# Two mixtures of experts in one kernel: routing weights spread by DMAs that repeat a DRAM row, and inputs laid out by the host

## What is computed

```python
x = x + tanh(g_xattn[0]) * strided_cross_attention(layernorm(x), ctx)         # 16 heads
x = x + tanh(g_ffn[0])   * (attention + mixture_0)(layernorm(x))
x = x + tanh(g_xattn[1]) * bidirectional_match(layernorm(x), ctx)
x = x + tanh(g_ffn[1])   * mixture_1(layernorm(x))

# mixture_0: 8 experts, hidden width 256, best two by softmax, and a shared expert
combine = sum(one_hot(topi, 8) * softmax(topw))
spec = einsum('etd,te->td', (silu(gate) * up) @ e_down, combine)
out = X + swiglu(h2, sh_gate, sh_up, sh_down) + spec
# mixture_1: 16 experts, hidden width 64, best two, weights summed to 1
y = sum(y_sel * scores)
y = y + sigmoid(xt @ Wsg.T) * (silu(xt @ Ws_gate.T) * (xt @ Ws_up.T)) @ Ws_down.T
```

## Time and profile before

| | us |
|---|---|
| three runs | 495.77, 496.0, 497.8 (median 496.0) |
| span of the profiled execution | 494.2 |
| PE busy | 453.3 |
| DVE busy | 358.1 |
| POOL busy | 319.0 |
| ACT busy | 287.7 |
| DMA queue of SP and ACT, share of 16 engines' span | 6.9% and 0.2% |

### The profile page before, as it was taken

One profiled execution on the slowest core, in us unless ns is written; L12 is line 12 of the kernel. 1 busy time (PEld: TensorE's weight loads), 2 busy tenths in 40 slices (PEclk: granted clock), 3 DMA queues, 4 the chain that ended last, 5 costly groups with the idle time before them and its releaser, 6 DMA issues.

```text
span 494.2 us, 11017 instructions
## 1 busy us (share of the span) xinstructions
PE 453.3 (92%) x3724; PEld 341.0 (69%) x3724; DVE 358.1 (72%) x930; ACT 287.7 (58%) x559; POOL 319.0 (65%) x525
## 2 busy tenths in 40 slices
PE   6859888999999999999999999899989997899996
PEld 5646555676677777677767877686858775687674
DVE  4657877899988878968656747775766756877864
ACT  2424566766787774565674476536664477446452
POOL 7895889898868676546934584547635573446553
PEclk9988999999999999999999999999999999999999
DMA  6340000040101000020000000000000000000000
GB/s 164 79 140 2 0 3 3 1 119 5 56 3 57 1 1 0 1 55 0 2 1 0 2 1 1 0 0 0 0 0 1 2 1 0 23 1 23 0 23 21
DMA packets 19353, 9.80 MB, mean 20 GB/s; under 512 B 6535, under 2 KB 18792, under 8 KB 19304
## 3 DMA queue, kind: packets, MB, share of 16 engines
q1 hardware_dynamic: 18584, 9.04, 6.9%
q10 hardware_dynamic: 720, 0.13, 0.2%
HBM read 8.12 MB, written 1.05 MB: 19 GB/s over the span
## 4 chain that ended last, share of the span: by engine, by line
PE 49%; POOL 18%; DVE 14%; issue 13%; ACT 4%; POOLq 1%; ACTq 0%; DVEq 0%
PE PS L1774 9%; PE PS L1776 9%; PE PS L1775 8%; POOL HLO L618 3%; DVE work L1382 2%; PE PS L1700 2%; PE PS L1694 2%; PE PS L1930 2%; DVE work L1387 2%; PE PS L1689 2%; PE PS L1662 2%; PE PS L1734 2%; POOL rs L437 1%; DVE RDT L1135 1%; PE PS L1677 1%
## 5 line engine op out<-in xcount | busy, mean ns | idle before, releaser
L618 POOL TENSOR_TENSOR HLO<-work,HHI 128x512 fp32r<-128x512 f32 x111 | 143.1, 1292 | 128.2 <-ACT HHI L869 124.8
L876 ACT ACTIVATE work<-PS 128x512 f32<-128x512 f32 x112 | 66.8, 596 | 91.1 <-PE PS L1776 88.4
L1382 DVE TENSOR_TENSOR work<-work,PS 128x512 f32<-128x512 f32 x104 | 71.0, 683 | 57.3 <-ACT work L876 32.3
L1387 DVE TENSOR_TENSOR work<-PS,work 128x512 f32<-128x512 f32 x112 | 77.2, 691 | 19.2 <-POOL HLO L618 10.8
L869 ACT ACTIVATE HHI<-work 128x512 fp32r<-128x512 f32 x111 | 69.8, 629 | 29.3 <-DVE work L1387 29.1
L1099 DVE TENSOR_REDUCE nmax<-PS 128x4 f32<-128x512 f32 x64 | 42.2, 683 | 8.3 <-PE PS L1662 7.9
L738 ACT ACTIVATE EX<-PS 128x512 f32<-128x512 f32 x64 | 35.0, 603 | 12.3 <-PE PS L1677 12.1
L1774 PE MATMUL PS<-HHI,W0H_down 128*128 128x512 f32 x72 | 35.0, 485 | 0.2
L1774 PE MATMUL PS<-H2H,W0H_gate 128*128 128x512 f32 (+1 forms) x72 | 32.0, 444 | 0.7 <-ACT work L876 0.7
L1930 PE MATMUL PS<-CWT,sel 128*128 128x512 bf16 (+1 forms) x68 | 26.5, 390 | 6.5 <-DVE work L1382 6.0
L1774 PE MATMUL PS<-H2H,W0H_up 128*128 128x512 f32 (+1 forms) x72 | 29.2, 406 | 2.9 <-DVE work L1387 2.9
(11 more groups left out here) (355 smaller groups left out, 1204.3 us busy)
## 6 DMA issues: line engine op xcount, KB each, us to landing
X<-in_x_dram SPq DMA_DIRECT2D x4, 256.0 KB, 5.2
raw<-in_L_ffn_e_gate_dram SPq DMA_DIRECT2D x1, 1024.0 KB, 5.5
raw<-in_L_ffn_e_up_dram SPq DMA_DIRECT2D x1, 1024.0 KB, 7.2
out_dram<-X SPq DMA_DIRECT2D x3, 256.0 KB, 2.3
raw<-in_L_ffn_We_gate_dram SPq DMA_DIRECT2D x1, 512.0 KB, 4.0
raw<-in_L_ffn_We_up_dram SPq DMA_DIRECT2D x1, 512.0 KB, 3.9
raw<-in_L_ffn_We_down_dram SPq DMA_DIRECT2D x1, 512.0 KB, 4.1
ctx_nat<-in_ctx_dram SPq DMA_DIRECT2D x1, 462.0 KB
```

The lines of the kernel that those rows point to most:

```text
L618: pool.tensor_tensor(HLO[t][:], HH[k % 2][:], HHI[t][:].bitcast(F32), ALU.subtract).then_inc(m_sem["lo"], 1)
L876: act.activation(SG[c % 2][:], PS[:, c % 2, :], ACT.Silu).then_inc(S["silu"], 1)
L1382: dve.tensor_tensor(SG[c % 2][:], SG[c % 2][:], PS[:, 4, :], ALU.mult).then_inc(S["scaled"], 1)
L1387: dve.tensor_tensor(HH[c % 2][:], PS[:, 2 + c % 2, :], SG[c % 2][:], ALU.mult).then_inc(S["hid"], 1)
```

## The change

**Spreading.** The pieces, the selectors and the selector products are gone. PE transposes `comb` itself in float32 (8 or 17 rows x 512), ACT copies it to one tile `CW`, SP stores it to a DRAM tensor `WD[m]`, and for each use SP issues a DMA of 128 x 512 floats (256 KB) that repeats a DRAM row into a ring of four tiles `BCW` in SBUF. DVE's scaled multiply reads `BCW` instead of PSUM. For a pair of experts the source is two rows, each repeated 64 times. The shared expert of the first mixture now comes first (`weights_of`, chunks 0 and 1, `UNWEIGHTED`), the eight experts after it.

```diff
+RING = 4
+    UNWEIGHTED = (2, 0)
+    WD = [nc.dram_tensor(f"WD{m}", (G, E, GT), F32) for m, E in enumerate((E0, E1 + 1))]
...
-        CS = sb("CS", [P, B, P], BF16)
-        sel0 = sb("sel0", [P, E0, P], BF16)
-        sel1 = sb("sel1", [P, NC1 + 1, P], BF16)
+        CW = sb("CW", [E1 + 1, GT])
+        BCW = [sb(f"BCW{r}", [P, GT]) for r in range(RING)]
...
+            def store_rows(m, g):
+                sp.wait_ge(r_sem[m]["ct_sb"], g + 2)
+                sp.dma_start(WD[m][g], CW[0:(E0, E1 + 1)[m], :]).then_inc(rows_out, 16)
+
+            def spread_weights(m, g):
+
+                sp.wait_ge(rows_out, 16 * (m * G + g + 1))
+                for e in range(NBC[m]):
+                    k = g * NBC[m] + OFF[m][2] + e
+                    if k >= RING:
+                        sp.wait_ge(m_sem["scaled"], last_use(k - RING) + 2)
+                    if m == 0:
+                        what = WD[0][g, e:e + 1, :].broadcast_to([P, GT])
+                        sp.dma_start(BCW[k % RING][:], what).then_inc(spread[k % RING], 16)
+                    elif e < NC1:
+                        what = WD[1][g, 2 * e:2 * e + 2, :].unsqueeze(1).broadcast_to([2, F1, GT])
+                        sp.dma_start(BCW[k % RING][:], what).then_inc(spread[k % RING], 16)
+                    else:
+                        what = WD[1][g, E1:E1 + 1, :].broadcast_to([P, GT])
+                        sp.dma_start(BCW[k % RING][:], what).then_inc(spread[k % RING], 16)
...
+                else:
+                    store_rows(0, 0)
+                    spread_weights(0, 0)
+                    store_rows(0, 1)
+                    sp.wait_ge(turn_lo, 3)
...
+            store_rows(0, 2)
+            store_rows(0, 3)
+            spread_weights(0, 1)
+            spread_weights(0, 2)
+            store_rows(1, 0)
+            spread_weights(0, 3)
+            store_rows(1, 1)
+            spread_weights(1, 0)
             for g in range(G - 1):
+                spread_weights(1, g + 1)
+                if g + 2 < G:
+                    store_rows(1, g + 2)
                 sp.wait_ge(m_sem["x"], G + g + 2)
...
-                    if c < NSC[m]:
-                        e = min(c // per, (n - 2) // per)
-                        dve.wait_ge(S["bc"], g * NBC[m] + OFF[m][2] + e + 2)
-                        dve.tensor_tensor(SG[c % 2][:], SG[c % 2][:], PS[:, 4, :], ALU.mult).then_inc(S["scaled"], 1)
+                    if c >= UNWEIGHTED[m]:
...
+                        dve.wait_ge(spread[r], 16 * uses)
+                        dve.tensor_tensor(SG[c % 2][:], SG[c % 2][:], BCW[r][:], ALU.mult).then_inc(S["scaled"], 1)
...
-                        ins = pe.transpose(PS[:, 5, :].bitcast(BF16)[:, j * P:(j + 1) * P], CS[:, j, :], identb[:])
+                        ins = pe.transpose(PS[0:E1 + 1, 5, j * P:(j + 1) * P], comb[:, j, 0:E1 + 1], identf[:])
```

```diff
-                sp.dma_start(X[:, g * GB:(g + 1) * GB, :], a["x"][g * GB:(g + 1) * GB].rearrange("b s d -> s b d")).then_inc(x_in[g], 16)
+                sp.dma_start(X[:, g * GB:(g + 1) * GB, :], a["x"][:, g * GB:(g + 1) * GB, :]).then_inc(x_in[g], 16)
...
-                sp.dma_start(ctx_nat[:, at, :], a["ctx_1024"][at].rearrange("b s d -> s b d")).then_inc(ctx_in[k], 16)
+                sp.dma_start(ctx_t[:, at, :], a["ctx_turned"][:, at, :]).then_inc(ctx_in[k], 16)
...
-            pe.wait_ge(wkv_in, 16 * 2)
-            for i in range(2):
-                ins = pe.transpose(PS[:, 0, i * D:(i + 1) * D], w_nat[:, i, :], identf[:])
```

More of the change, by code:

```diff
@@ L76, in build @@
         tg = sb("tg", [P, 4])
-        bq_c, bk_c, bv_c, n1w, n2w, w1_c, w2s, w3s = (
-            sb(n, [P, 1]) for n in ("bq_c", "bk_c", "bv_c", "n1w", "n2w", "w1_c", "w2s", "w3s"))
+        columns = sb("columns", [P, 8])
+        bq_c, bk_c, bv_c, n1w, n2w, w1_c, w2s, w3s = (columns[:, k:k + 1] for k in range(8))
         bo_r = sb("bo_r", [P, D])
@@ L234, in turn_of, with weights_of, load_of @@
             return (c if m == 0 else g * NCH[1] + c) % LAG
[L236 to L242, removed]
+        def weights_of(m, c):
+            return (c - 2) % NCH[0] if m == 0 else c
+        def load_of(m, c):
+            return (c - 2) // 2 if m == 0 else min(c, NC1)
         def mixtures(eng, chunks, first_steps, second_steps, matching):
@@ L266, in side, with turns @@
             return g % 2 if m == 0 else 0
-        def turns(g, turn, n=10):
-            return [(c, turn(t)) for t, (of, c) in enumerate(TURN_AT[:n]) if of == g]
+        def turns(g, turn):
+            return [(c, turn(t)) for t, (of, c) in enumerate(TURN_AT) if of == g]
         def routed(p):
@@ L374, in _ @@
                 at = slice(B - GB + 2 * k, B - GB + 2 * k + 2)
[L375 removed]
+                sp.dma_start(out[:, at, :], X[:, at, :]).then_inc(out_done, 16)
             sp.wait_ge(out_done, 16 * (G + 1))
@@ L1759, in turn_tokens, with turn_weights @@
                 ins.then_inc(R["t"], 1)
-            def turn_weights(k, bank, lo, n):
+            def turn_weights(k, bank):
                 pe.wait_ge(r_sem[0]["cs"], 2 if k == 0 else 3)
-                if k == 2:
-                    pe.wait_ge(r_sem[0]["ct_sb"], 3)
-                for j in range(n):
-                    ins = pe.transpose(PS[:, bank, :].bitcast(BF16)[:, j * P:(j + 1) * P], CS[:, lo + j, :], identb[:])
+                if k >= 2:
+                    pe.wait_ge(r_sem[0]["ct_sb"], k + 1)
+                for j in range(GB):
+                    ins = pe.transpose(PS[0:E0, bank, j * P:(j + 1) * P], comb[:, k * GB + j, 0:E0], identf[:])
                 ins.then_inc(r_sem[0]["ct"], 1)
@@ L2057 @@
     arrays, args = {}, {}
-    for name in _INS:
-        v = _np.ascontiguousarray(inputs[name])
+    for name, what in laid_out({n: _np.asarray(v) for n, v in inputs.items()}).items():
+        v = _np.ascontiguousarray(what)
         arrays[f"in_{name}_dram"] = v
         args[name] = nc.dram_tensor(f"in_{name}_dram", v.shape, _mybir.dt.from_np(v.dtype), kind="ExternalInput").ap()
-    out = nc.dram_tensor("out_0_dram", (B, P, D), _mybir.dt.float32, kind="ExternalOutput").ap()
+    out = nc.dram_tensor("out_0_dram", (P, B, D), _mybir.dt.float32, kind="ExternalOutput").ap()
     build(nc, args, out)
     r = _run(nc, [arrays], core_ids=[0])
-    return r.results[0]["out_0_dram"]
+    return _np.ascontiguousarray(r.results[0]["out_0_dram"].transpose(1, 0, 2))
```

343 lines of the change are left out of this document (122 added, 221 removed).

## The result

The changed kernel took 569.88 us (median of 4 runs, 569.65 to 570.85) beside 495.99 for the kernel before (4 runs, 495.77 to 497.8): ratio 1.149, 95% interval 1.147 to 1.151. The profiled span is 567.9 us, where it was 494.2. The forecast was 544 us, with a range of 524 to 590.

The account below looks back on a forecast made before the run. PE (92% busy) bounds the kernel before; after the change narrow spreads pace the second mixture. 343 to its first spread + 178 + 9 + 12.5 = 542.5, with 1.8 around the span: 544 us, range 524 to 590.

Parts of the forecast that it names:

- The narrow spreads: Second mixture's 32 pair spreads, outermost dimension 2, use two engines and take 5.5 us each against 2.1 a chunk; chance 0.86.
- the deal inferred from a 77-row load: A transfer goes to a number of engines dividing its outermost dimension: 11 for 77 rows, 16 for 128, 2 for pairs.
- the signs named beforehand: Second mixture: pitch 5.5 us, DMA share near 0.13, 45 to 50 GB/s; first mixture: no DMA waits where nothing is inserted.
- The sum from the first narrow spread to the end: From 343 us on: 178 for spreads, 9 for the last group's weights, 12.5 to the end, giving 542.5.
- Its start: First narrow spread, after chunk 11 of the last first-mixture group frees its ring slot: 353.7 less 15.9 plus 5, 343 us.
- the savings of 15.9: Gains before the first narrow spread: products 6.9, waits 3.0, transposes 3.3 - 1.0, piece waits 0.7, POOL's selectors 3.0 us.
- the port: DVE's multiply with both inputs in SBUF and POOL's subtraction exclude each other: 10 us, half before the second mixture.
- the transposes: 30 transposes of the second mixture's weights on PE go, 0.11 us each: 3.3 us saved.
- the selectors: POOL's selectors go; PE waited for POOL's QS three times in self-attention: 3.0 us saved.
- the first rival: All spreads run at full width, about 2.1 us each, with 10 us for the port: 482 us; chance 0.10.
- the second's: Full width, but POOL's subtraction slips ahead of the next multiply, a loop of 3.3 us a chunk: 503 us; chance 0.04.
- The third: Pair spreads narrow and dear, 7.4 us each as in the 8 us stretch: 605 us; chance 0.05.

Follow-up runs that it names:

- e1_halves: The changed kernel with each pair's spread issued as two DMAs of 64 rows instead of one with outermost dimension 2: 496.97 us, ratio to before 1.0004.
- e3_four: The changed kernel with each pair spread repeating four DRAM rows 32 times each (outermost dimension 4): 503.59 us.
- e2_order: The changed kernel with the spreads of the second mixture's first group issued before the store of its second group's weights: 559.10 us.
- e9_narrow_psum: The changed kernel, narrow pair spreads kept, with silu written to PSUM for the weighted chunks, so DVE's multiply has one input there: 557.18 us.
- e7_layout: The kernel before with the host's new layout alone, no input transposes on PE; pieces, selectors and selector products as before: 494.88 us, ratio 0.9963.
- e5_psum: e1_halves with silu written back to PSUM for weighted chunks, so DVE's multiply has one input there: 479.01 us, ratio to before 0.965.

## Why the prediction was right, and where it was off

**The narrow spreads: right.** With an outermost dimension of 2 a 256 KB spread went at the pace that was forecast for two of sixteen engines; full width undid it (e1_halves), and four rows halved the pitch (e3_four). Three settings of the outermost dimension agree with the deal inferred from a 77-row load in the earlier trace rows: 5.27 us at 2, 2.64 at 4, no pitch at 16. The deal itself, and the 11 engines read out of 0.71 x 16, stay the author's estimate: no trace here tells one engine from another. Forecast was 5.5, from 23.9 GB/s an engine; 131 KB in 5.27 us is 24.9, if two engines share the 256 KB. (The lower bound speaks of a share of 1.07; the earlier trace rows has 1.08 there, and 5.0 us holds by it as well.) Of the signs named beforehand, the pitch, the share of 0.14, the 51 GB/s and DVE's some 3 us of wait a chunk came as said. That the first mixture would be free of DMA waits did not quite (3.79 us once), and its groups of experts did not get 3 us shorter.

**The sum from the first narrow spread to the end: right, in part by luck.** 542.5 - 343 = 199.5 us forecast, 567.9 - 369.84 = 198.1 measured. In it 32 x 0.23 = 7.4 less for the transfers, and 14.87 - 5.27 = 9.6 at the last group for a forecast 9. Not forecast were 458.19 to 467.71 between the second and the third group, 4.2 over a pitch, since the 17-row store stood behind narrow spreads, and a slower way from the issue of the first spread at 369.84 to its multiply at 378.31, 8.5 us where 5.5 + 1.6 were counted. That 7.4 us too much and nearly as much too little add up to 1.4 is chance.

**Its start: wrong, and the whole miss.** "The first narrow spread waits for the ring slot that chunk 11 of the last first-mixture group frees": 343 forecast, 369.84 measured, 26.8 us, against 25.4 by which the span was over. Two causes. First, 15.9 us: SP's program has `store_rows(1, 1)` ahead, and the step counted neither that store nor the wait on it (e2_order). The diff shows it; of a step that stands in an engine's program, everything ahead of it must be read. Even without the store, only 10.8 of the 15.9 us come back in the time, since the ring's tiles come free more slowly than 5.27 us there, which the forecast did not count either, and the store then stands behind narrow spreads. Second, 10.9 us: the savings of 15.9 up to there and the port's 5 came out as nothing at all (366.46 against 366.23 for the same transposes). At the second mixture's first gate product the savings came to 14.0 us and the port took 13.9 (e9_narrow_psum). So the term that was off is above all the port's, 5 us for 13.9. The savings fall short by 1.9, and that is about what the prologue became longer with the new layout (57.93 for 56.09), a term that the forecast put at 0. The terms of the sum that can be read held: the transposes gave 3.2 of 3.3 (e7_layout), the selectors some 3.6 for 3.0 (from the first QM copy to the first gate product 159.86 - 57.93 = 101.9 us, before 161.61 - 56.09 = 105.5). These readings are good to about 1 us: the first gate product stands between 159.16 and 160.29 in kernels that are the same up to there.

**The port: right in kind, half in size.** 10 us were forecast at full width, 18.0 measured (e1_halves less e5_psum), and before the second mixture 5 were forecast and 13.9 measured. I had put it near its lower bound, arguing from 1.98 us of port time a chunk under PE's 2.10. But here the hold did more than fill slack: the multiply is on the way from silu to the hidden product, and it took up to 1.1 us more (1.78 for 0.69). One place shows how that reached PE's next up product, when DVE had just been busy with an inserted step: behind the inserted steps at 191 to 196 us PE's gate products start at 193.04, 197.42, 201.03 and 203.13, two chunks of 4.4 and 3.6 us before the pace of 2.1 is back, while in e9_narrow_psum the same chunks take 2.4 and 2.2 (191.22, 193.66, 195.83). After PE's waits of 0.96 and 1.76 us there, its products from 197.42 on start 0.43 us apart, at a granted clock of 0.50 from 197.4 to 199.0 us, and 0.23 apart again from 200.33 on; in e9_narrow_psum the granted clock is 1.00 from 190 to 204 us. So more than the waits is lost there. How the 18 us divide over such places was not measured. That the two exclude each other was the author's inference from the earlier trace rows; the multiplies of up to 1.78 us and their end after POOL's (by 0.56 us at 352 us) agree with it, and so does its absence as soon as one input is in PSUM (maximum 0.692 us).

**The rivals.** At full width the kernel takes 497.0 us: neither the first rival's 482 nor quite the second's 503, and nearer to the second. e5_psum comes near the first's number (479.0), but the first had 10 us for the port in it: without them it says 472, and 7 us of the savings at full width did not come. Some 2 of the 7 are the prologue's; DVE's wait of 6.4 us for the last group's weights, of which PE feels 3.8 where 2.4 were counted, is another 1; the rest is open. The second's loop shows for a chunk or two behind an inserted step and then ends, as its own counter-argument has it. The third, 7.4 us a spread, did not come.

## What to carry to other kernels

Read the outermost dimension of the source of every large DMA, and not only the rows of its destination: a pattern of "two rows, each 64 times" says the same as two DMAs of 64 rows each, but took 5.27 us a transfer, where the two DMAs kept up with a chunk of 2.1 us. Replacing a product by a transfer also moves an operand from PSUM to SBUF. Where GpSimd reads SBUF in the same chunk, try one operand of the vector operation in PSUM, here by letting the activation write back where it read: it was worth 18.0 us at full width (e5_psum), and the longest multiply fell from 1.78 us in the changed kernel to 0.69. Read everything that stands ahead of a transfer in its engine's program: one store that waited held the first pair spread back by 15.9 us (e2_order). And a layout that makes loads simpler can still make the prologue longer, here by 1.6 us (e7_layout); look at its first waits before calling it free.

## What was not expected of the hardware

- The issue of a DMA took SP 4.88 us in the median (L330, outermost dimension 2), against 0.50 with 4 and 0.32 for a repeated row at full width. A repeated row at full width behind narrow ones took 5.12 (L333), and 0.33 when all were at full width (e1_halves). So here SP was held about as long as a transfer's pitch of 5.27 us, and all that it would issue next with it.
- A store of 34 KB took 9.9 us from its issue to the issue of the spreads that wait for it, with narrow spreads ahead in its queue, 6.8 from ACT's queue, and 2.98 with no spread in flight.
- PE's granted clock fell to 0.73 of full speed in the stretch from 520 to 541 us, where it was busy 14.0 of 21.0 us; its products start 0.23 us apart right behind an idle wait of 2.8 us at 379.78, and 0.43 apart from 381.39 on, at a granted clock of 0.50 (381.4 to 384.5 us). DVE's multiplies stayed 5.27 us apart through it, so it cost nothing to be seen there.
